# Second attention of a two-layer block: one stream of query pairs through all heads, scores split between groups of transposes, the value products in two blocks, quadrants added by VectorE, the division moved behind the attention

## The reference, cut to what matters

```python
l2 = jnp.sqrt(jnp.sum(x * x, axis=1, keepdims=True))
xn = x / jnp.maximum(l2, 1e-12) * g * float(c) ** 0.5
qkv = jnp.einsum('oc,bchw->bohw', w_qkv, xn)
q, k, v = jnp.split(qkv, 3, axis=1)
q, k, v = (rs(q) * scale, rs(k), rs(v))          # heads of 32 channels
sim = jnp.einsum('bhdi,bhdj->bhij', q, k)
attn = jax.nn.softmax(sim, axis=-1)
out = jnp.einsum('bhij,bhdj->bhdi', attn, v)
return jnp.einsum('oc,bchw->bohw', w_out, out) + b_out[None, :, None, None] + x
```

## Time and profile before

| | |
|---|---|
| median of 3 runs | 5868.32 us (5866.23 to 5868.85) |
| profiled execution, its own time | 5872.33 us |
| its span | 5870.2 us |
| mean granted TensorE clock of the span | 0.819 |
| busy share of the span: PE, DVE, ACT, POOL | 74%, 74%, 74%, 26% |

### The profile page before, as it was taken

One profiled execution on the slowest core, in us unless ns is written; L12 is line 12 of the kernel. 1 busy time (PEld: TensorE's weight loads), 2 busy tenths in 40 slices (PEclk: granted clock), 3 DMA queues, 4 the chain that ended last, 5 costly groups with the idle time before them and its releaser, 6 DMA issues. The chain is left out here.

```text
span 5870.2 us, 115806 instructions
## 1 busy us (share of the span) xinstructions
PE 4366.5 (74%) x32459; PEld 2810.7 (48%) x32459; DVE 4365.0 (74%) x25530; ACT 4327.3 (74%) x6804; POOL 1500.0 (26%) x362
## 2 busy tenths in 40 slices
PE   7565566666676366666666666998999999999998
PEld 4343344444444244444444444435556556655655
DVE  4888888888888888888888887313577777777775
ACT  2787799888898588988899889342567666666765
POOL 0343344443444244434444444001000000000000
PEclk8676677777777677777777777998999999999999
DMA  5000000000000000000000000102210101001012
GB/s 188 6 16 14 6 15 16 7 15 15 7 16 15 4 15 10 12 15 14 8 15 15 7 15 14 41 7 101 93 29 21 29 20 30 20 21 28 22 28 82
DMA packets 79588, 154.72 MB, mean 26 GB/s; under 512 B 8120, under 2 KB 49464, under 8 KB 73528
## 3 DMA queue, kind: packets, MB, share of 16 engines
q1 hardware_dynamic: 78904, 146.72, 8.8%
HBM read 99.50 MB, written 47.19 MB: 25 GB/s over the span
## 5 line engine op out<-in xcount | busy, mean ns | idle before, releaser
L565 DVE MAX8 a_top<-a_scores 128x8 f32<-128x36 f32 x18432 | 1829.3, 180 | 254.9 <-ACT a_scores L446 254.5
L547 POOL TENSOR_TENSOR a_probs<-a_scores,a_probs 128x2304 f32<-128x2304 f32 x288 | 1458.1, 5084 | 2081.7 <-ACT a_probs L462 2081.7
L373 PE MATMUL a_ps_t<-ident,a_probs 128*128 128x128 f32 x5184 | 976.8, 326 | 1045.4 <-ACT a_probs_t L457 685.8
L373 PEld LDWEIGHTS a_ps_t<-ident,a_probs 128*128 128x128 f32 x5184 | 675.4, 164 | 1333.9 <-ACT a_probs_t L457 865.0
L1108 PE MATMUL b_ps_t<-ident,b_soft 128*128 128x128 f32 x5184 | 795.2, 286 | 97.2 <-ACT b_soft_t L1181 68.7
L462 ACT ACTIVATE a_probs<-a_scores,a_steep_kth 128x2304 f32<-128x2304 f32 x290 | 641.1, 2211 | 294.1 <-DVE a_minus_max L671 294.1
L1193 DVE TENSOR_SCALAR_CACHE_REDUCE b_soft<-b_ps_s 128x2304 f32<-128x2304 f32 x290 | 741.6, 2557 | 89.0 <-PE b_ps_s L1095 70.1
L1181 ACT ACTIVATE b_soft_t<-b_ps_t 128x512 f32<-128x512 f32 (+1 forms) x864 | 438.0, 525 | 488.4 <-PE b_ps_t L1108 487.7
L1108 PEld LDWEIGHTS b_ps_t<-ident,b_soft 128*128 128x128 f32 x5184 | 558.6, 142 | 450.2 <-issue 304.1
L457 ACT ACTIVATE a_probs_t<-a_ps_t 128x512 f32<-128x512 f32 (+1 forms) x1440 | 725.7, 546 | 18.2 <-PE a_ps_t L373 6.8
L363 PE MATMUL a_ps_s<-a_k_stack,a_q_ring 128*128 128x512 f32 (+1 forms) x1465 | 652.2, 605 | 13.5 <-ACT a_scores L446 8.9
(11 more groups left out here) (126 smaller groups left out, 4420.7 us busy)
## 6 DMA issues: line engine op xcount, KB each, us to landing
a_k_stack<-k_parts SPq DMA_DIRECT2D x72, 288.0 KB, 5.9
b_k_stack<-k_parts SPq DMA_DIRECT2D x72, 288.0 KB, 6.0
a_q_ring<-q_parts SPq DMA_DIRECT2D x294, 64.0 KB
b_q_ring<-q_parts SPq DMA_DIRECT2D x294, 64.0 KB
k_parts<-p_high SPq DMA_DIRECT2D x36, 256.0 KB, 2.1
k_parts<-p_rest SPq DMA_DIRECT2D x36, 256.0 KB, 2.1
q_parts<-p_high SPq DMA_DIRECT2D x36, 256.0 KB, 2.0
q_parts<-p_rest SPq DMA_DIRECT2D x36, 256.0 KB, 2.0
```

What stands on the lines that cost most here:

```text
L373: last = pe.transpose(ps_t[(NTG * s + g) % 2][:, P * m:P * m + P], probs[s % 2][:, P * (m0 + m):P * (m0 + m) + P], cst["ident"][:, :])
L547: pool.tensor_tensor(probs[u][:, :], scores_all[:, 2 * (p % 2) + u, :], probs[u][:, :], ALU.subtract).then_inc(masked_ready, 1)
L565: last = dve.max(top8[s // 2 % 2][:, s % 2, c, :], scores_all[:, s % 4, CHUNK * c:CHUNK * c + CHUNK])
```

## The change

- `attention_full`: the loop over heads now runs 7 times and its body is pairs 2 to 19, counted on into the next head, so that no head is drained; the first two pairs stand ahead of the loop, the last sixteen behind it, and only the last pair of all is drained.
- PE's order is now written for a pair (`pair_step`). The scores of each later tile are split: two chunks and three chunks, with group 1 of transposes between, for the first tile; one and four for the second. The `weigh` groups stand in two blocks, 0 to 2 (24 instructions) and 3 to 4 (12).
- ACT takes the exponentials of tile s + 2 right behind group 4 of tile s, and `keep_parts` stands ahead of the last group's copy.
- The quadrants: PE turns `parts` with two transposes (`turn_parts`) in place of the four product instructions, and DVE adds four quadrants by one `tensor_reduce` of 128 x 256 to 128 x 64 straight into `o_all`.
- The sums of all tiles and heads are kept (288 columns in the space of `xs`, which is free by then), so that DVE's reciprocals (two for a pair) and the multiplication go. In `output` DVE takes one reciprocal of 128 x 288 and multiplies each chunk of `o_all`, 128 x 1024, by it (`divide`). PE's `turn(c)` waits for it. `divide(0)` and `divide(1)` come first, `divide(c + 2)` behind both additions of chunk c.

```diff
-            with pe.Fori(0, HEADS) as h:
-                for p in range(HEAD_PAIRS):
-                    pair = h * HEAD_PAIRS + p
-                    for u in range(2):
-                        s, tile = 2 * p + u, h * HEAD_TILES + 2 * p + u
-                        pe.wait_ge(soft_ready, tile + 1)
-                        turn(s, 0, tile)
-                        turn(s, 1, tile)
-                        if u == 0 and p > 1:
-                            add_quadrants(pair - 2)
-                        score(s + 2, h, tile + 2)
-                        for g in range(2, NTG):
-                            if p > 0 and 2 * u + g - 2 < 2 + 3 * u:
-                                weigh(p - 1, 2 * u + g - 2, pair - 1, h)
-                            turn(s, g, tile)
-                add_quadrants(h * HEAD_PAIRS + HEAD_PAIRS - 2)
-                for g in range(NTG):
-                    weigh(HEAD_PAIRS - 1, g, h * HEAD_PAIRS + HEAD_PAIRS - 1, h)
-                add_quadrants(h * HEAD_PAIRS + HEAD_PAIRS - 1)
+            def pair_step(p, h, before=2, ahead=True):
+
+                pair, tile, s = h * HEAD_PAIRS + p, h * HEAD_TILES + 2 * p, 2 * p
+                turn(s, 0, tile)
+                if before > 1:
+                    turn_parts(pair - 2)
+                if ahead:
+                    score(s + 2, h, tile + 2, range(0, 2))
+                turn(s, 1, tile)
+                if ahead:
+                    score(s + 2, h, tile + 2, range(2, 5))
+                turn(s, 2, tile)
+                turn(s, 3, tile)
+                if before > 0:
+                    for g in range(3):
+                        weigh(p - 1, g, pair - 1, h)
+                turn(s, 4, tile)
+                turn(s + 1, 0, tile + 1)
+                if ahead:
+                    score(s + 3, h, tile + 3, range(0, 1))
+                turn(s + 1, 1, tile + 1)
+                if ahead:
+                    score(s + 3, h, tile + 3, range(1, 5))
+                turn(s + 1, 2, tile + 1)
+                turn(s + 1, 3, tile + 1)
+                if before > 0:
+                    for g in range(3, NTG):
+                        weigh(p - 1, g, pair - 1, h)
+                turn(s + 1, 4, tile + 1)
...
+            for p in range(2):
+                pair_step(p, 0, before=p)
+            with pe.Fori(0, HEADS - 1) as h:
+                for p in range(2, HEAD_PAIRS + 2):
+                    pair_step(p, h)
+            for p in range(2, HEAD_PAIRS):
+                pair_step(p, HEADS - 1, ahead=p < HEAD_PAIRS - 1)
...
@@ vector @@
-            def finish(p, h, pair):
+            def add_quadrants(p, h, pair):
+
+                ahead, p = divmod(p, HEAD_PAIRS)
                 dve.wait_ge(added, pair + 1)
-                dve.wait_ge(inverse_ready, 2 * pair + 2)
...
+                dve.tensor_reduce(o_all[:, 2 * p:2 * p + 2, cols((h + ahead) * D, D)],
+                                  ps_o[:, PAIR:2 * PAIR].rearrange("p (u q d) -> p u d q", u=2, q=4),
+                                  AX.X, ALU.add).then_inc(o_ready, 1)
+            def pair_step(p, h, before=2, ahead=True):
+                pair, tile, s = h * HEAD_PAIRS + p, h * HEAD_TILES + 2 * p, 2 * p
+                if before > 1:
+                    add_quadrants(p - 2, h, pair - 2)
                 for u in range(2):
...
+                    for g in range(BY_DVE):
+                        keep_turned(s + u, g, tile + u)
+                    if ahead:
+                        shift(s + 2 + u, tile + 2 + u)
...
@@ output, vector @@
+            def divide(c):
+                o_c = o_all[:, 4 * c:4 * c + 4, :].rearrange("p m (h d) -> p m h d", d=D)
+                inverse_c = one_by_sum[:, 4 * c:4 * c + 4, :].unsqueeze(3).to_broadcast([P, 4, HEADS, D])
+                dve.tensor_tensor(o_c, o_c, inverse_c, ALU.mult).then_inc(divided, 1)
+
+            dve.reciprocal(one_by_sum[:, :, :], sums[:, :, :]).then_inc(inverse_ready, 1)
+            dve.wait_ge(inverse_ready, 1)
+            divide(0)
+            divide(1)
...
+                if c + 2 < NCH:
+                    divide(c + 2)
```

More of the change, by code:

```diff
@@ L1081, in _, with score @@
             pe.sem_inc(parts_ready, 1)
-            def score(s, h, tile, first=False):
+            def score(s, h, tile, chunks=range(len(SCOLS)), first=False):
                 ahead, s = divmod(s, HEAD_TILES)
                 b, pair = s // MCH, s // 2
[L1087 to L1094, removed]
+                if chunks[0] == 0:
+                    if s % 2 == 0:
+                        pe.wait_ge(q_loaded[pair % AHEAD_Q],
+                                   (h + ahead) * (32 * HEAD_PAIRS // AHEAD_Q) + 32 * (pair // AHEAD_Q + 1))
+                    if s % MCH == 0:
+                        pe.wait_ge(k_loaded[b], (h + ahead) * 64 + 64)
+                    if not first:
+                        pe.wait_ge(shifted_ready, tile)
+                for chunk in chunks:
+                    c, n = SCOLS[chunk]
                     last = pe.matmul(ps_s[:, c:c + n], q_ring[pair % AHEAD_Q][:, P * (s % 2):P * (s % 2) + P],
                                      k_stack[b][:, c:c + n], start=True, stop=True)
-                last.then_inc(scores_done, 1)
+                if chunks[-1] == len(SCOLS) - 1:
+                    last.then_inc(scores_done, 1)
             def turn(s, g, tile):
+                if g == 0:
+                    pe.wait_ge(soft_ready, tile + 1)
                 if g < BY_DVE:
@@ L1129, in weigh, with turn_parts @@
                     last.then_inc(weighed, 1)
-            def add_quadrants(pair):
+            def turn_parts(pair):
                 pe.wait_ge(parts_ready, pair + 2)
@@ L1162, in _, with exponentials @@
+            with pe.Fori(0, HEADS - 1) as h:
[3 more added lines that the diff above has]
+                pair_step(p, HEADS - 1, ahead=p < HEAD_PAIRS - 1)
+            turn_parts(ALL_PAIRS - 2)
+            for g in range(NTG):
+                weigh(HEAD_PAIRS - 1, g, ALL_PAIRS - 1, HEADS - 1)
+            turn_parts(ALL_PAIRS - 1)
         @block.scalar
         def _(act):
-            def exponentials(s, tile):
+            def exponentials(s, h, tile):
+                ahead, s = divmod(s, HEAD_TILES)
@@ L1171, in keep_parts, with pair_step @@
                 act.activation(parts[:, :], ps_o[:, 0:PAIR], ACT.Copy).then_inc(parts_ready, 1)
[L1173 to L1186, removed]
+            def pair_step(p, h, before=1, ahead=True):
+                pair, tile, s = h * HEAD_PAIRS + p, h * HEAD_TILES + 2 * p, 2 * p
+                exponentials(s + 1, h, tile + 1)
+                for g in range(BY_DVE, NTG):
+                    keep_turned(s, g, tile)
+                if ahead:
+                    exponentials(s + 2, h, tile + 2)
+                for g in range(BY_DVE, NTG - 1):
+                    keep_turned(s + 1, g, tile + 1)
+                if before > 0:
+                    keep_parts(pair - 1)
+                keep_turned(s + 1, NTG - 1, tile + 1)
+            exponentials(0, 0, 0)
+            for p in range(2):
+                pair_step(p, 0, before=p)
+            with act.Fori(0, HEADS - 1) as h:
+                for p in range(2, HEAD_PAIRS + 2):
+                    pair_step(p, h)
+            for p in range(2, HEAD_PAIRS):
+                pair_step(p, HEADS - 1, ahead=p < HEAD_PAIRS - 1)
+            keep_parts(ALL_PAIRS - 1)
         @block.vector
@@ L1225, in output @@
-def output(nc, cst, o_all, x1, w_out, b_out, out):
+            for p in range(2):
+                pair_step(p, 0, before=p)
+            with dve.Fori(0, HEADS - 1) as h:
+                for p in range(2, HEAD_PAIRS + 2):
+                    pair_step(p, h)
+            for p in range(2, HEAD_PAIRS):
+                pair_step(p, HEADS - 1, ahead=p < HEAD_PAIRS - 1)
+            for p in (HEAD_PAIRS - 2, HEAD_PAIRS - 1):
+                add_quadrants(p, HEADS - 1, (HEADS - 1) * HEAD_PAIRS + p)
@@ L1226, in output @@
+def output(nc, cst, o_all, sums, x1, w_out, b_out, out):
     CW = BANK
@@ L1336, in build @@
             project_heads(nc, xs, mlp_weights.next_w, mlp_weights.next_loaded, operands, q_parts, k_parts, v_all)
[L1337 to L1338 removed]
+            attention_full(nc, cst, operands, q_parts, k_parts, v_all, o_all, sums)
+        output(nc, cst, o_all, sums, x1, t["w_out"], t["b_out"], out)
 def per_partition(v, rows=P):
```

50 lines of the change are left out of this document (24 added, 26 removed).

## The result

| | before | changed |
|---|---|---|
| median | 5867.59 us (4 runs, 5866.23 to 5868.85) | 5590.39 us (4 runs, 5588.13 to 5594.08) |
| ratio | | 0.9528, 95% interval 0.9512 to 0.9545 |
| span of the profiled execution | 5870.2 us | 5586.0 us |

The change saves 277 us. The direction and the places were right; the sizes of three terms were not.

What follows compares the result with a forecast made beforehand. The prediction took PE to set the pace, with a tenth of waiting. From 5872.3 us, pairs -226, seams -25 and output stage +32 gave 5653 on the profiled execution, 5650 us predicted; range 5600 to 5725.

Steps and rivals of the forecast that it cites:

- PE's work for a pair: PE's instructions in one pair, summed from trace rows: 9.06 us against 9.94 before; 9.1 taken.
- Steady pair: Ordinary pair: 9.1 us of work plus 0.3 of waiting, 9.4 against 10.99; 226 us saved over 142 distances.
- The cause of today's waits: PE's 1.05 us of waiting a pair: ACT's copies come late behind the exponentials and the two-bank ring.
- The ring of scores and shifts: One set of score banks makes shifts and scores alternate: 8.9 us a pair, just shorter than PE's 9.1.
- Seams: Between heads: six loop ends remain at 5.8 us each, 35 us in all against 60.5; 25 saved.
- the 2.5 us for the clock: Part of each seam's 5.8 us: PE's lowered clock behind a loop end costs 2.5 us.
- Output stage: Divisions between additions and projections put projections 6.56 us apart: 32 us lost, bounds +20 and +54.
- The 12 us for a lower clock: Part of the output stage's loss: PE's new 2.1 us gaps may lower its clock, a third of 34 us.
- rival 2: PE runs without waits at full clock, a pair at 9.1 us or a little under: 5595 to 5610 us; chance 0.16.
- Rival 1: Shift ring, ACT or switches with waits set the pace, a pair at 9.7 to 10.5: 5693 to 5806 us; chance 0.20.
- rival 3: PE waits as much longer as its work shrinks, a pair stays at 10.9 to 11.0: 5875 us; chance 0.03.
- rival 4: DVE's reduction is slow and lengthens the ring; at 2.3 us the time is 5906 us; chance 0.03.

Runs made afterwards that it cites:

- e3: Changed kernel with the quadrants added by PE's four product instructions again and a 128x64 copy on DVE: 5608.6 us, 9.22 us a pair.
- e1: Changed kernel with the five score chunks of a tile unsplit again, behind groups 0 and 1: 5617.9 us, 9.35 us a pair.
- e2: Changed kernel with the value products in five blocks as before, not two: 5784.2 us, 10.52 us a pair.
- e11: Changed kernel with both weigh blocks behind group 4's transposes and ACT's partial results behind its last copy: 5722.9 us, 10.03 us a pair.
- e9: Changed kernel with ACT's copy of the partial results behind its last group's copy, as before the change: 5666.5 us, 9.65 us a pair.
- e6: Changed kernel without value group 2 in each ordinary pair, so part of the keys is missing: 5564.3 us, 8.94 us a pair.
- e5: Changed kernel with DVE's sum of quadrants made twice, the first into a spare tile: 5623.0 us, 9.33 us a pair.
- e4: Changed kernel with every head started and drained by itself as before, order within a pair as changed: 5620.2 us.
- e7: Changed kernel with all nine divisions ahead of the additions in the output stage: 5570.2 us.
- e8: As e7, and the loops over heads on PE, ACT and DVE run over bodies of two heads: 5550.4 us.

## Why the prediction was wrong

Direction, order of the terms and their places held. By its steps:

- *PE's work for a pair*: 9.06 forecast, 9.11 measured, 0.08 of it a wait for DVE (e3). The row-by-row sum was right to a percent, the cost of splitting near nothing (e1).
- *Steady pair, the failing step*: "I put back 0.3 us of waiting where PE's order and the ring meet". Measured: 9.11, with 0.08 of waiting in it. 142 x 0.29 = 41 us, the greater part of the 60 missed. The 1.05 us of waiting in the kernel before had two named places, and I carried a third of it over without asking, of each, whether its cause was still there. The traces show both gone: the block of 24 stands between groups 3 and 4, so that group 0 no longer follows close on the group whose bank it needs (e2, e11), and chunks of scores stand ahead of group 1 (e1). A third wait would have come with the change, and the new order on ACT keeps it out (e9, 0.53); it got no term in the prediction.
- *The cause of today's waits* was misread as well. The prediction has ACT's copies late "because the exponentials and the two-bank ring stand in front of them". Only the ring does. ACT's rows in the pair of the earlier trace rows show it idle, waiting for PE, ahead of both copies, and the exponentials in front had ended two and three microseconds earlier, at 4813.05 and 4818.19:

```profile
4815.13 0.87 ACT L1181 ACTIVATE b_soft_t<-b_ps_t 128x512 f32<-128x512 f32 x2 [0.56 <-PE b_ps_t L1108]
4821.19 0.38 ACT L1181 ACTIVATE b_soft_t<-b_ps_t 128x256 f32<-128x256 f32 x1 [0.33 <-PE b_ps_t L1108]
```

  What PE waited for is the way through a bank itself, transposes, copy, next transposes, with too little of PE's own work beside it. PE's own order can fill that, and did: in the changed pair ACT's copies of groups 2 and 3 do stand behind an exponential and start at 4806.88, yet the block of 24 lasts until 4808.66 and covers them.
- *The ring of scores and shifts*: 8.9 forecast, 8.94 in e6. It didn't set the pace. The reduction takes 0.425 us in 126 rows of the loop, where 0.5 was assumed; by e5 another 0.34 us costs 0.22 a pair, so 0.5 in place of 0.42 would have cost some 0.05, an estimate. The Trainium skill, VectorE: DVE Perf Modes, "Rules for kernel authors", which calls this operation the slowest, would have spoken against moving it to DVE; here DVE is busy for 8.04 of the 9.11 us, and the trace has the reduction within about 0.01 us of a copy of as many elements from PSUM.
- *Seams*: 25 saved forecast, 34 measured. The wait behind the loop end, 3.1 to 3.5 (19.5 for six), was right. The term that failed is the 2.5 us for the clock, read from one head, which had the lowest clock over six microseconds of all seven seams before (0.50; the others 0.51 to 0.77). In the changed kernel the clock was 0.59 to 0.68 over 3.4 us behind five loop ends and full behind one, which costs 1.1 a seam on the average; so a seam cost 27.1 / 6 = 4.5 and not 5.8. e4 confirms the sum: 36.0.
- *Output stage*: +32 forecast, +21 measured. The gap between projections, 6.51 against 6.56, was right. The 20.4 us for the chain of addition, division and transposes was right too. The 12 us for a lower clock failed: with PE idle for 1.98 in every 6.51 us, the clock stayed at full level for five projections in a row (3.60 us each). It was low at the start of the stage, as before the change, behind the 7.11 us wait for the residual (a projection of 4.47 us) and near the end. All that comes to about 1 us (21.3 less 20.4). e7 shows the rest: moved to the front, the divisions cost nothing.
- *Rivals*: rival 2, no waits and a full clock at 5595 to 5610, is in the main what happened, and it had 0.16; the cheaper seams put the time 5 us below it. Rival 1 (a pair at 9.7 or more), the unchanged pair (rival 3) and the slow reduction (rival 4) are out.

The lower end of the range, 5600, lay inside rival 2's own 5595 to 5610. The bounds I had written down myself, 9.1 for the pair (43), 40 for the seams (15) and +20 for the output (12), lead to 5650 - 43 - 15 - 12 = 5580.

Open: what decides how long the clock is down behind a loop end. It was about three microseconds behind most in the changed kernel, nothing behind one, and nearly six behind both in e8, with the same order of work and about the same idle time in front. And what the quadrants and the kept sums are worth without the changes of order.

## What to carry over

When the order of a full engine is rewritten, sum its instructions from starts in the trace, and then go through each of today's waits by name, with the rows of the engine that is waited for: a wait whose cause has been covered is worth nothing in the new sum, and a share of it put back "for safety" is an error with a sign. The place of a long block matters as much as its size: put it in front of the instruction whose bank another engine is still emptying, as the same blocks one place later brought a wait of 0.4 to 0.5 us in each tile (e11). When an instruction is moved forward, ask also what it will now wait for (e9). And work moved "to the end" should go to where its engine waits for something else, not between two steps of a chain.

## What I had not expected of the hardware

- After PE had been idle for 3.1 to 3.5 us at a loop end, the clock was low for about three microseconds behind five seams of the changed kernel, and not at all behind one. Gaps of 1.98 us, one in every 6.5, mostly left it at 2.4 GHz, while a wait of 0.91 us near the end of a head was followed by the 1.2 GHz level in the kernel before.
- A loop body twice as long didn't slow the pairs inside it: the ordinary pairs of e8 take 9.11 us. The two seams that are left cost 6.0 us each, where six had cost 4.5 to 4.9 on the average, and the granted clock accounts for it (0.53 over six microseconds).
- A wait of 0.48 us by starts can show as 0.31 of idle time (e9), and one of 0.25 as none (e6), because PE's instructions overlap.
